# Norms, high parts, a copy and a maximum placed anew on ScalarE and VectorE in an attention and FP4 gate kernel

## The reference

```
s = LN2(y1 + gelu(y1*W1 + b1)*W2 + b2),  y1 = LN1(xn + attention(xn))
attention: Q = elu(q)+1, K = elu(k)+1, KV = sum K v, Z = 1/(Q . sum K + eps), o = Q KV Z, times Wo
f = quantized(silu(gate) * up) * w_down,  gate and up from xn quantized to FP4 in blocks of 16
out = x + s * silu(f)
```

## Time and profile before

| | |
|---|---|
| median of 3 runs | 1679.24 us |
| profiled execution | 1680.37 us, span 1678.5 us |
| TensorE busy | 1644.1 us, 98% |
| VectorE busy | 1322.8 us, 79% |
| ScalarE busy | 967.5 us, 58% |
| GpSimd busy | 778.4 us, 46% |
| granted TensorE clock | 0.996 of full speed |

### The profile page before, as it was taken

How to read it: one execution, slowest core, us unless ns; L and a number is a source line. 1 busy time by engine, 2 the same in 40 slices (tenths; PEclk the granted TensorE clock), 3 DMA queues, 4 the chain that set the end, 5 groups by cost and what they waited for, 6 DMA issues and landing times.

```text
span 1678.5 us, 30547 instructions
## 1 busy us (share of the span) xinstructions
PE 1644.1 (98%) x11105; PEld 1469.2 (88%) x11105; DVE 1322.8 (79%) x2587; ACT 967.5 (58%) x1754; POOL 778.4 (46%) x718
## 2 busy tenths in 40 slices
PE   7999999999999999999999999999999999999997
PEld 6878888888889898989999998989898999999897
DVE  6685664555879797979889797979797988979797
ACT  6665656655464646565655556464646565555644
POOL 4564543434134444444453534444444446353446
PEclk9999999999999999999999999999999999999999
DMA  7322323422200101021010102010101201010100
GB/s 230 130 77 89 106 66 116 121 91 91 93 1 1 51 1 51 19 86 52 1 51 2 51 2 104 2 51 2 51 19 34 77 29 51 1 51 2 51 1 26
DMA packets 69986, 89.36 MB, mean 53 GB/s; under 512 B 8383, under 2 KB 54603, under 8 KB 68814
## 3 DMA queue, kind: packets, MB, share of 16 engines
q1 hardware_dynamic: 69838, 87.42, 15.9%
HBM read 53.30 MB, written 34.10 MB: 52 GB/s over the span
## 4 chain that ended last, share of the span: by engine, by line
PE 54%; DVE 12%; issue 4%; ACT 1%; POOL 1%; DVEq 0%; ACTq 0%
PE QH L81 7%; PE QH L83 6%; PE QH L82 6%; PE AC L81 6%; PE AC L83 6%; PE AC L82 6%; PE GU L81 4%; PE GU L83 4%; PE GU L82 4%; PE TT L816 3%; DVE hb L1760 1%; DVE bslna L1840 1%; DVE hb L1758 1%; PE QH L714 1%; DVE AC L1831 1%
## 5 line engine op out<-in xcount | busy, mean ns | idle before, releaser
L1212 ACT ACTIVATE rh<-QH 128x512 fp32r<-128x512 f32 x256 | 147.1, 595 | 84.2 <-DVE QH L1918 80.1
L81 PE MATMUL GU<-wgh,xqh 128*128 128x352 f32 x512 | 171.2, 334 | 8.9 <-DVE hb L1760 8.8
L2416 POOL TENSOR_TENSOR hb<-hb,rs_h 128x704 f32<-128x704 f32 x64 | 89.1, 1392 | 170.0 <-DVE rs_h L1767 170.0
L82 PE MATMUL GU<-wgl,xqh 128*128 128x352 f32 x512 | 165.7, 324 | 0.0
L83 PE MATMUL GU<-wgh,xql 128*128 128x352 f32 x512 | 165.6, 323 | 0.0
L1933 DVE TENSOR_TENSOR rl<-QH,rh 128x512 fp32r<-128x512 f32 x128 | 85.7, 689 | 95.1 <-ACT rh L1212 74.7
L81 PE MATMUL AC<-Mh,rh 128*128 128x256 f32 x512 | 145.7, 285 | 0.0
L81 PE MATMUL AC<-w2h,rh 128*128 128x256 f32 x512 | 144.2, 282 | 0.0
L82 PE MATMUL AC<-Ml,rh 128*128 128x256 f32 x512 | 142.8, 279 | 0.0
L83 PE MATMUL AC<-Mh,rl 128*128 128x256 f32 x512 | 142.7, 279 | 0.0
L82 PE MATMUL AC<-w2l,rh 128*128 128x256 f32 x512 | 142.4, 278 | 0.0
(11 more groups left out here) (241 smaller groups left out, 5711.1 us busy)
## 6 DMA issues: line engine op xcount, KB each, us to landing
xa<-in_L_attn_src SPq DMA_DIRECT2D x16, 512.0 KB, 4.2
xt_scratch<-xth SPq DMA_DIRECT2D x32, 256.0 KB, 2.6
xt_scratch<-xtl SPq DMA_DIRECT2D x32, 256.0 KB, 3.0
xb<-in_L_attn_src SPq DMA_DIRECT2D x16, 512.0 KB, 4.2
xnTh<-xt_scratch SPq DMA_DIRECT2D x32, 256.0 KB, 4.7
xnTl<-xt_scratch SPq DMA_DIRECT2D x32, 256.0 KB, 5.4
out<-x SPq DMA_DIRECT2D x15, 512.0 KB, 6.6
m_scratch<-mh SPq DMA_DIRECT2D x16, 256.0 KB, 2.4
```

The lines of the kernel that those rows point to most:

```text
L81: e.matmul(outp, lh, rh, start=start, stop=False, skip_group_check=check)
L82: e.matmul(outp, lh, rl, start=False, stop=False, skip_group_check=check)
L1212: e.activation(RH[j % 4][:], src, ACT.Copy).then_inc(S[sem], 1)
L2416: e.tensor_tensor(hb, hb, spread(rs_h[i % 2][:], 44), ALU.mult).then_inc(S["hin"], 1)
```

## The change

- `z_sign` leaves ScalarE. `den_inverse` on VectorE makes `zhi` itself with one `tensor_scalar` more.
- `h_max(a)` leaves its place in front of `den_inverse` and comes after `z_lo(.,0)`, right before `h_scale(a)`.
- `ln1_norm` of the tiles 0 and 1 becomes two activations on ScalarE, after `gate_tanh(c,0)` and before `x1_hi`. They need a bias, minus mean times reciprocal deviation, which GpSimd makes with two small operations more in `ln1_rstd` of the first pair. The tiles 2 and 3 stay on VectorE, now behind `gate_mul(c,0)` and no longer in front of it.
- On ScalarE `gelu_hi(.,5)` and `gelu_hi(.,6)` come right after their gelus. Before, `gelu(5)`, `gelu(6)`, `h_abs(d)` and `x_norm(2)` came first.
- On VectorE `gelu_lo(.,5)` comes before `x_max(.,0)` from the second group on and in the first.
- The semaphore `lnan` is split: it counts ScalarE's norms, `lnad` counts VectorE's.

```diff
 TensorE
-                w.wait_ge(S["lnan"], 4 * g + 4)
+                w.wait_ge(S["lnan"], 2 * g + 2)
+                w.wait_ge(S["lnad"], 2 * g + 2)
...
-                w.wait_ge(S["lnan"], 4 * g + 2 * pr + 2)
+                if pr:
+                    w.wait_ge(S["lnad"], 2 * g + 2)
+                else:
+                    w.wait_ge(S["lnan"], 2 * g + 2)
 ScalarE
-            def z_sign(g):
-                w.wait_ge(S["zi"], 2 * g + 2)
-                w.wait_ge(S["sel"], 6)
-                w.wait_ge(S["zd"], 4 * g)
-                e.activation(zhi[:], dn_s[:], ACT.Identity, scale=sg[:, 1:2]).then_inc(S["zc"], 1)
+            def ln1_norm(g, t):
+                w.wait_ge(S["lnap"], 2 * g + 1)
+                w.wait_ge(S["lnab"], g + 1)
+                e.activation(x1[g % 2][:, t, :], AC[:, t * D:(t + 1) * D], ACT.Identity, bias=nmb1[:, t:t + 1],
+                             scale=rsb["lna"][:, t:t + 1]).then_inc(S["lnan"], 1)
...
                 gate_tanh(a + 4, 0)
-                z_sign(g + 1)
                 gate_tanh(b + 4, 0)
...
                 gate_tanh(c + 4, 0)
+                ln1_norm(g + 1, 0)
+                ln1_norm(g + 1, 1)
                 x1_hi(g + 1, 0)
...
                 gelu(g + 1, 5)
+                gelu_hi(g + 1, 5)
                 gelu(g + 1, 6)
+                gelu_hi(g + 1, 6)
                 h_abs(d + 4)
                 if g + 2 < NG:
                     x_norm(g + 2, 2)
-                gelu_hi(g + 1, 5)
 VectorE
-            def ln1_norm(g, pr):
-                w.wait_ge(S["lnap"], 2 * g + pr + 1)
-                for t in (2 * pr, 2 * pr + 1):
+            def ln1_norm(g):
+
+                w.wait_ge(S["lnap"], 2 * g + 2)
+                for t in (2, 3):
                     e.tensor_scalar(x1[g % 2][:, t, :], AC[:, t * D:(t + 1) * D], mvb["lna"][:, t, 0:1], rsb["lna"][:, t:t + 1],
-                                    ALU.subtract, ALU.mult).then_inc(S["lnan"], 1)
+                                    ALU.subtract, ALU.mult).then_inc(S["lnad"], 1)
...
                 e.reciprocal(dn_s[:], dn_s[:]).then_inc(S["zi"], 1)
+                w.wait_ge(S["zi"], 2 * g + 2)
+                w.wait_ge(S["sel"], 6)
+                e.tensor_scalar(zhi[:], dn_s[:], sg[:, 1:2], None, ALU.mult).then_inc(S["zc"], 1)
...
+                gelu_lo(g, 5)
                 x_max(g + 1, 0)
-                gelu_lo(g, 5)
...
                 gate_mul(a + 4, 0)
-                h_max(a + 4)
                 den_inverse(g + 1)
...
                 z_lo(g + 1, 0)
+                h_max(a + 4)
                 h_scale(a + 4)
...
                 ln1_stats(g + 1, 1)
-                ln1_norm(g + 1, 0)
-                ln1_norm(g + 1, 1)
                 gate_mul(c + 4, 0)
+                ln1_norm(g + 1)
 GpSimd, in ln1_rstd
+                if pr == 0:
+                    e.tensor_tensor(nm1[:], mvb["lna"][:, tiles, 0], neg4[:, 0:2], ALU.mult).then_inc(S["lnam"], 1)
+                    w.wait_ge(S["lnap"], 2 * g + 1)
+                    w.wait_ge(S["lnam"], g + 1)
+                    e.tensor_tensor(nmb1[:], nm1[:], rsb["lna"][:, tiles], ALU.mult).then_inc(S["lnab"], 1)
```

More of the change, by code:

```diff
@@ L52 @@
     "x1Tl", "gel", "lna", "lnb", "fin",
-    "hin", "hout", "xin", "xout", "lnap", "lnbp", "lnav", "lnbv", "lnbs", "us", "xab", "xnb", "vb2", "half", "fo", "lastp",
+    "hin", "hout", "xin", "xout", "lnap", "lnam", "lnab", "lnad", "lnbp", "lnav", "lnbv", "lnbs", "us", "xab", "xnb", "vb2", "half", "fo", "lastp",
     "wraw", "wk0", "wk1", "bk", "wgr0", "wgr1", "wgr2", "wdr", "vec", "row", "wqr", "wv", "x0", "x1", "x2", "m0", "m1", "ksr", "ksl", "kst", "xb0", "xb1", "xs0", "xs1", "xtl", "mld", "out0", "out1",
@@ L198, in build @@
         Xb = [Xb0, sb("xb1", [128, 4, D])]
-        sb("main_rest", [128, 682])
+        nm1, nmb1 = sb("nm1", [128, 2]), sb("nmb1", [128, 2])
+        sb("main_rest", [128, 678])
         A2 = ExitStack()
@@ L1387, in _ @@
             gate_tanh(0, 0)
-            z_sign(0)
             gate_tanh(1, 0)
@@ L1405, in _ @@
             gate_tanh(2, 0)
+            ln1_norm(0, 0)
+            ln1_norm(0, 1)
             x1_hi(0, 0)
@@ L1427, in _ @@
             gelu(0, 5)
+            gelu_hi(0, 5)
             gelu(0, 6)
+            gelu_hi(0, 6)
             h_abs(3)
             x_norm(1, 2)
-            gelu_hi(0, 5)
-            gelu_hi(0, 6)
             g_tanh(1)
@@ L1451, in _ @@
             gate_tanh(4, 0)
-            z_sign(1)
             gate_tanh(5, 0)
@@ L1476, in _ @@
             gate_tanh(6, 0)
+            ln1_norm(1, 0)
+            ln1_norm(1, 1)
             x1_hi(1, 0)
@@ L1498, in _ @@
             gelu(1, 5)
+            gelu_hi(1, 5)
             gelu(1, 6)
+            gelu_hi(1, 6)
             h_abs(7)
             x_norm(2, 2)
-            gelu_hi(1, 5)
             for g in range(1, NG - 1):
                 a, b, c, d = 4 * g, 4 * g + 1, 4 * g + 2, 4 * g + 3
-                gelu_hi(g, 6)
                 g_tanh(b)
@@ L1576, in _ @@
                     x_norm(g + 2, 2)
-                gelu_hi(g + 1, 5)
             g_tanh(NT - 3)
-            gelu_hi(NG - 1, 6)
             h_hi(NT - 2, 0)
@@ L1835, in ln1_stats @@
                 w.wait_ge(S["lnap"], 2 * (g - 1) + pr + 1)
-                w.wait_ge(S["lnan"], 4 * (g - 1) + 2 * pr + 2)
+                if pr:
+                    w.wait_ge(S["lnad"], 2 * g)
+                else:
+                    w.wait_ge(S["lnab"], g)
                 w.wait_ge(S["lna"], v + 1)
@@ L2113, in _ @@
             gate_mul(0, 0)
-            h_max(0)
             den_inverse(0)
@@ L2121, in _ @@
             z_lo(0, 0)
+            h_max(0)
             h_scale(0)
@@ L2147, in _ @@
             ln1_stats(0, 1)
-            ln1_norm(0, 0)
-            ln1_norm(0, 1)
             gate_mul(2, 0)
+            ln1_norm(0)
             xT_half(0, 0, "x1T", "x1Th", "x1Tl")
@@ L2168, in _ @@
             h_round(2)
+            gelu_lo(0, 5)
             x_max(1, 0)
-            gelu_lo(0, 5)
             gelu_lo(0, 6)
@@ L2195, in _ @@
             gate_mul(4, 0)
-            h_max(4)
             den_inverse(1)
@@ L2203, in _ @@
             z_lo(1, 0)
+            h_max(4)
             h_scale(4)
@@ L2232, in _ @@
             ln1_stats(1, 1)
-            ln1_norm(1, 0)
-            ln1_norm(1, 1)
             gate_mul(6, 0)
+            ln1_norm(1)
             xT_half(1, 0, "x1T", "x1Th", "x1Tl")
@@ L2439, in ln1_rstd @@
                 w.wait_ge(S["lna"], 10 * g + 5 * pr + 5)
-                w.wait_ge(S["lnan"], 4 * (g - 1) + 2 * pr + 2)
+                if pr:
+                    w.wait_ge(S["lnad"], 2 * g)
+                else:
+                    w.wait_ge(S["lnan"], 2 * g)
                 w.wait_ge(S["cp"], 5)
```

## The result

The changed kernel takes 1686.34 us (median of 5 runs, 1684.92 to 1686.78) against 1679.24 before: the ratio is 1.0037, with an interval of 1.0026 to 1.0048. It is slower, by 6 to 7 us (6.2 by the ratio, 7.1 by the two medians), and lies above the predicted range. The profiled execution took 1686.56 us, its span is 1684.8.

The account below looks back on a forecast made before the run. TensorE, busy 98% of the span, was taken as the bound, with 1.7 us a group of idle to win. Groups -0.8, first -0.8, last -0.3 make -1.9: 1677.3 us against the 1679.24 median, range 1668.5 to 1684.

Parts of the forecast that it names:

- the sum: Whole kernel: 15 groups by -0.05 are -0.8, first group -0.8, last -0.3, together -1.9 us.
- Copy, 0.36 with its waits: VectorE's copy of the reciprocals replaces a 0.55 us round trip over ScalarE: 0.36 with waits, a gain of 0.19.
- The maximum, +0.91 on VectorE, +0.39 at turn_xq: Later maximum in front of h_scale costs VectorE 0.91 us; TensorE's turn_xq starts 0.39 later than before.
- Rival (a): Later maximum isn't felt by TensorE: a group gains 0.6 us, 9 in all, giving 1670; chance 0.28.
- Norms and gate product, -0.35 at gate_up(d,0): Two norms go to ScalarE, VectorE's other two follow the gate product: gate_up(d,0) starts 0.35 us earlier.
- place 3: TensorE's wait at h_proj(7) for a low part, 0.45 us a group; claimed to go.
- rival (d): ScalarE's norms 0.8 late, turn_x1(0) the new wait: +0.35 us a group, 1682.5; chance 0.06.
- GpSimd's chain: Gapless GpSimd work from h_round(c) to q_proj(3) gives back nearly all of the 0.45 us won at h_proj(7).
- Rival (c): h_scale(c) waits for GpSimd's port, low part 2 delays h_proj(4): 6 us more, 1683.3; chance 0.13.
- The -0.8 of the first group: First group, no down product before z_spread: 0.47 counts directly, 0.35 more before gate_up(d,0), -0.8 us.
- the -0.3 of the last: Last group has no next x to quantize, so it keeps some of the gain at h_proj(7): -0.3 us.

Follow-up runs that it names:

- e9: Changed kernel with filler main_rest cut from 678 to 672 columns, so operands lie where they did in the kernel before: 1679.61 us, ratio 1.0011.
- e11: Changed kernel with the maximum back ahead of the reciprocals and main_rest at 672 columns, operands in their old places: 1668.42 us, ratio 0.9941.
- e14: Kernel before with both the weights and x1 to hql moved up by 32 bytes: 1679.16 us, one run.
- e6: Changed kernel with all four parts undone, keeping the three new semaphores, two small tensors and cut filler: 1685.20 us, ratio 1.0029.
- e10: Kernel before with main_rest at 690 columns in place of 682, moving x1 to hql up by 32 bytes: 1685.20 us, ratio 1.0041.
- e12: Kernel before with a 32-byte gap ahead of rh0, moving only rh, rl, hqh and hql: 1682.00 us, one run.
- e13: Kernel before with only the weights moved up by 32 bytes: 1687.60 us, one run.
- e8: Changed kernel once more, unaltered, against the kernel before on the same chip: 1685.26 us, ratio 1.0034.

## Why the prediction was wrong

**The step that failed** is, in the main, none of those in the sum: it is a term that wasn't there. The part-by-part list costs the copy, the maximum, the norms and the high parts, and nothing for the new small tensors and the filler. They cost 0.32 to 0.34 us a group, not by themselves but by moving the matmuls' operands by 32 bytes (77.88 to 78.20 with the kernel before, 77.85 to 78.19 with the changed one; of the 0.7 of lost pace the other half goes into stalls that VectorE and ScalarE set anyway, most plainly the one ahead of h_proj(7), which the earlier trace rows show). Over 15 groups that is 5 us: 1677.3 + 5 is 1682. Of the sum's -1.9 another 1.6 didn't come (see the sum below), which makes 1684, inside the interval of the ratio (1683.6 to 1687.3); the rest to 1686 isn't accounted for.

**The steps that were costed.** The changed kernel in the old places (e9) is the one that my sum describes. Shifts of TensorE's starts inside a group against the kernel before, medians over 13 groups (a gate_up by its second matmul, the last row by the mean):

| step | predicted | e9 | changed kernel |
|---|---|---|---|
| gate_up(b,1) | -0.49 | -0.43 | -0.43 |
| turn_xq | +0.39 | +0.45 | +0.50 |
| gate_up(d,0) | +0.20 | +0.20 | +0.25 |
| behind h_proj(7) | -0.25 | -0.25 | +0.24 |
| q_proj(3) | -0.06 to 0 | -0.08 | +0.23 |
| next group | -0.05 | -0.02 | +0.32 |

- *Copy, 0.36 with its waits.* Right: 0.29 at 907.34, the z parts 0.32 behind its start.
- *The maximum, +0.91 on VectorE, +0.39 at turn_xq.* Right in size (0.45 in e9); the wait is shared with the z_spread in front. Rival (a), that it isn't felt, falls: e11 against e9 is (a) made real. I had priced it at 0.6 us a group; it is 0.78.
- *Norms and gate product, -0.35 at gate_up(d,0), and place 3 gone.* Right, both by their amount. ScalarE's two norms end at 935.02, 0.45 ahead of turn_x1, so rival (d) falls.
- *GpSimd's chain takes the gain of place 3 back at q_proj(3).* Right. In e9 the shift goes from -0.25 to -0.08 there, and q_proj(3) starts just behind the end of q_elu(1) (965.05 + 0.68), as in the earlier trace rows. VectorE and TensorE in e9:

```profile
965.05 0.68 DVE L1753 SCALAR_TENSOR_TENSOR Q<-QH,eg 128x512 f32<-128x512 f32 x1
```

```profile
965.27 0.60 PE L821 MATMUL TT<-ident,hb 128*128 128x128 f32 x4
965.79 0.50 PE L81 MATMUL QH<-xnTh,wqh 128*128 128x512 f32 x1
```

In the changed kernel this wait isn't there, because lost pace had made TensorE later than the chain before it got there. Even at e11's -1.07 the chain takes only 0.2 to 0.3 back (-0.80 at the group's end): as a cap it was softer than I wrote.
- *Rival (c), h_scale(c) behind GpSimd.* It fell. VectorE and GpSimd in the changed kernel:

```profile
943.76 0.49 DVE L1771 TENSOR_SCALAR sn_h<-am_h 128x44 f32<-128x44 f32 x1
944.28 0.19 DVE L1773 TENSOR_SCALAR am_h<-sn_h 128x44 f32<-128x44 f32 x1
```

```profile
941.81 2.39 POOL L2526 TENSOR_TENSOR x<-Gb,x 128x1024 f32<-128x1024 f32 x1
944.28 2.44 POOL L2530 TENSOR_TENSOR x<-x,xb 128x1024 f32<-128x1024 f32 x1
```

The first scaling comes 0.44 us before the end (941.81 + 2.39 = 944.20) of a long operation and is over just behind it (944.25), and the second starts at the same 944.28 as the next long one and takes 0.19. The prediction had expected the second to take over 2 us. The 2.41 us of the earlier trace rows are gone: 15 of the 64 first scalings take over 1 us before and none in the changed kernel. They weren't on TensorE's path: in the second profile of the kernel before, 13 of the first and 2 of the second scalings are the long ones, and the group is the same to 0.01 us.
- *The sum.* -0.05 a group was nearly right (-0.02), so 15 groups give -0.3 and not -0.8. The -0.8 of the first group and the -0.3 of the last didn't come. With the operands in matching places the first group takes 76.43 in the old order (e14) and 76.74 in the new one (e9), with one side moved 76.80 (e6) and 76.92 (changed); from the last den_sums to the end it is 76.62 before and 76.65 in e9.

**What is left.** The median of e9 is 1.7 us above the kernel before (0.5 to 3.4 by the interval), where its groups ask for 0.3 below. A part of what differs between two profiles is the granted clock. In the two profiles of the kernel before, the same program, the start of the main stage differs by 1.9 us, and over all profiles by 3.7 (432.8 to 436.5 us), nearly all of it gathered between 40 and 58 us. Windows there and in the first group, of the kernel before (us, busy time of each engine, granted clock, DMA share, GB/s):

```profile
44.00:50.00 6.00, 6.00 (x38) 5.42 (x38) 1.69 (x9) 3.44 (x5) 3.00 (x5) 0.84 0.05 14
50.00:58.00 8.00, 8.00 (x35) 6.54 (x35) 4.51 (x5) 4.23 (x9) 3.80 (x4) 0.91 0.02 6
435.00:446.00 11.00, 9.15 (x76) 8.17 (x68) 9.05 (x19) 2.44 (x5) 1.39 (x1) 0.84 0.47 145
```

and of the changed kernel:

```profile
44.00:50.00 6.00, 6.00 (x34) 5.52 (x34) 1.44 (x8) 2.48 (x3) 2.99 (x5) 0.67 0.02 6
50.00:58.00 8.00, 8.00 (x31) 6.51 (x30) 4.65 (x5) 4.64 (x9) 2.35 (x3) 0.82 0.00 0
435.00:446.00 11.00, 9.24 (x108) 7.80 (x107) 9.19 (x20) 2.65 (x6) 0.67 (x1) 1.00 0.55 172
```

The clock is at its lower level (1.2 of 2.4 GHz) for part of these stretches, and for how long differs from run to run. Before the main stage that is 2.0 of the 6.2 us between the two spans. The other 4.2 are 0.31 in each of 14 groups, +0.5 behind the last den_sums and -0.7 in the first group. The -0.7 is no gain of the change: the kernel before spends part of its first group at the lower level (0.84 against 1.00) and takes 77.60 us for it, while the five kernels in the old order without such a stretch (e6, e10, e12, e13, e14) take 76.4 to 76.9.

The clock doesn't explain the medians. Every timed run has its mean granted clock on record: 0.9976 for the changed kernel against 0.9967 for the kernel before on the same chip (e8, 5 and 23 runs), and 0.9974 against 0.9975 for e9 (11 and 15 runs). So the 1.7 us of e9 stay open.

## What to carry to other kernels

An edit that adds or resizes a tensor can move every tensor placed behind it; list the addresses of matmul operands before and after, and pin them with a filler when only the order of work is to be compared. Where TensorE is busy longer with the same matmuls, compare the times from start to start at one step before any theory about waits, and run the old order with the new allocation, the one experiment that splits the two. Of the change itself three parts are worth taking and one is not: without the later maximum and with the old places the kernel takes 1668.4 us, 0.6% less than before, and the maximum should stay in the shadow of den_sums.

## What the runs showed of the hardware

- The pace of these fp32 matmuls on split operands can depend on where the operands lie in SBUF. On w2, wd and w1 256 columns took 114 to 116 ns from start to start where both operands lay 32 bytes above a multiple of 64, or both at one, and 117 to 119 with one of each; 512 columns took 228 to 230 and 232 to 235. It isn't a rule for all: Mh and Ml with rh stayed near 117 ns in both cases, and xnTh with wqh went from 233 to 231 only with both 32 above, not with both at a multiple of 64. The Trainium skill (TensorE: Matmul & The Clock Gate, "Part 2: What happens when you issue a matmul") says that TensorE has two independent read ports, so that loading the next weights takes nothing from the running matmul. If neither read cost the other anything, where the two lie against each other should not matter. In these runs it does, by up to 4%: a 32-byte move of either operand costs some 2 to 7 ns, and the measurement decides. Which of the two reads pays isn't seen in the trace.
- An operation of VectorE that waits for one of GpSimd got in at its end, ahead of the next GpSimd operation (0.49 us at 943.76), where one that came 0.06 us behind its start took 2.41. By these two the wait is what is left of the one GpSimd operation that is running.
